# Transposes of the state prefix collected into two runs per head group, in an eight-core attention and mixture-of-experts layer

## What is computed

```python
x = x + attn(layernorm(x));  x = x + ffn(layernorm(x))
# attn: 32 heads of 64, blocks of 256 tokens
q, k, v = split(silu(h @ qkv_w.T))
def step(state, blk):                     # scan over the blocks
    aw = einsum('id,jd->ij', qi, ki) * dd
    y  = aw @ vi + (qi * qd) @ state
    state = state * bd + (ki * kd).T @ vi
    return state, y
attn = sigmoid(h @ gate_w.T) * rmsnorm(ys) @ out_w.T
# ffn, for each of 7 experts and a shared one:
u = xt @ Wup + bup;  g = silu(u @ Wgate + bgate) * u
out += probs * (g @ Wdown + bdown)        # probs: softmax over the top 2
```

## Time and profile before

| | us |
|---|---|
| runs of the kernel | 4628.54 and 4684.06, median 4656.3 |
| the profiled execution | 4629.22 |
| its span, on core 5, the slowest | 4627.2 |
| spans of the eight cores | 4614.4 to 4627.2 |
| mean granted TensorE clock | 0.908 to 0.910 |
| one group of the attention (208.9 to 488.2) | 279.3 |

### The profile page before, as it was taken

How to read it: one execution, slowest core, us unless ns; L and a number is a source line. 1 busy time by engine, 2 the same in 40 slices (tenths; PEclk the granted TensorE clock), 3 DMA queues, 4 the chain that set the end, 5 groups by cost and what they waited for, 6 DMA issues and landing times.

```text
span 4627.2 us, 44136 instructions; the slowest of 8 cores (4614.4 to 4627.2 us)
## 1 busy us (share of the span) xinstructions
PE 3923.8 (85%) x18010; PEld 1748.3 (38%) x18010; DVE 827.4 (18%) x1373; ACT 593.8 (13%) x691; POOL 249.9 (5%) x477
## 2 busy tenths in 40 slices
PE   1386867769659954999999999999999999999996
PEld 0132332324214411444444444444444444444443
DVE  3313122230322234011011011011010010110012
ACT  3311111111121030110110100100100100100100
POOL 0000000000000000000000000000000000000000
PEclk9996876869659966999999999999999999999997
DMA  3211110121104311444444444444444444444443
GB/s 101 72 32 19 33 32 19 28 46 33 23 5 73 69 45 25 76 73 75 76 73 76 75 73 74 77 73 74 76 75 74 73 73 73 74 74 76 78 69 96
DMA packets 75331, 284.48 MB, mean 61 GB/s; under 512 B 9814, under 2 KB 9975, under 8 KB 71038
## 3 DMA queue, kind: packets, MB, share of 16 engines
q0 software_dynamic: 67216, 243.39, 31.2%
q1 hardware_dynamic: 7918, 38.29, 2.6%
HBM read 516.55 MB, written 8.39 MB: 113 GB/s over the span
## 4 chain that ended last, share of the span: by engine, by line
PE 82%; DVE 8%; issue 4%; ACT 3%; DMA 2%; DVEq 0%; ACTq 0%; SPq 0%; POOL 0%; POOLq 0%
PE PD L368 28%; PE PE L368 27%; PE PE L1041 10%; PE PD L1041 10%; PE PT L383 2%; DVE awT L640 2%; PE PC L654 1%; PE PE L654 1%; DVE statc L405 1%; PE PC L1077 1%; PE PC L812 1%; ACT R L447 1%; DMA ring<-i_wup 1%; ACT R L674 1%; PE PC L665 0%
## 5 line engine op out<-in xcount | busy, mean ns | idle before, releaser
L368 PE MATMUL PD<-R,ring 128*128 128x512 bf16 x5888 | 1323.8, 384 | 23.7 <-ACT R L998 10.8
L368 PE MATMUL PE<-R,ring 128*128 128x512 bf16 x5888 | 1300.8, 379 | 2.2 <-DMA ring<-i_wgt 1.2
L368 PEld LDWEIGHTS PD<-R,ring 128*128 128x128 bf16 x5888 | 577.8, 99 | 738.4 <-issue 70.5
L368 PEld LDWEIGHTS PE<-R,ring 128*128 128x128 bf16 x5888 | 575.7, 98 | 698.2 <-issue 5.6
L1041 PE MATMUL PD<-R,ring 128*128 128x512 bf16 x2048 | 463.2, 385 | 24.9 <-DVE R L1025 21.0
L1041 PE MATMUL PE<-R,ring 128*128 128x512 bf16 x2048 | 452.5, 379 | 1.6 <-DMA ring<-i_wdn 1.6
L1018 DVE TENSOR_TENSOR R<-R 128x1024 bf16<-128x1024 bf16 x128 | 88.6, 692 | 1629.7 <-ACT R L1011 1629.7
L1041 PEld LDWEIGHTS PD<-R,ring 128*128 128x128 bf16 x2048 | 201.7, 99 | 278.2 <-issue 46.6
L1041 PEld LDWEIGHTS PE<-R,ring 128*128 128x128 bf16 x2048 | 199.5, 98 | 245.6 <-issue 7.3
L998 ACT ACTIVATE R<-PD,bupP 128x1024 bf16<-128x1024 f32 x56 | 62.4, 1114 | 1052.6 <-PE PD L368 929.6
L383 PE MATMUL PT<-ident_b,R 128*128 128x128 bf16 x256 | 37.4, 300 | 154.8 <-ACT R L447 120.1
(11 more groups left out here) (168 smaller groups left out, 1626.6 us busy)
## 6 DMA issues: line engine op xcount, KB each, us to landing
ring<-i_wup POOLq DMA_DIRECT2D x112, 512.0 KB, 5.1
ring<-i_wgt POOLq DMA_DIRECT2D x112, 512.0 KB, 5.2
ring<-i_wdn POOLq DMA_DIRECT2D x112, 512.0 KB, 5.1
xstage<-i_xm SPq DMA_DIRECT2D x16, 1024.0 KB, 5.1
ring<-i_wk POOLq DMA_DIRECT2D x16, 512.0 KB, 5.7
xstage<-i_xp SPq DMA_DIRECT2D x8, 1024.0 KB, 5.6
ring<-i_wv POOLq DMA_DIRECT2D x16, 512.0 KB, 5.7
ring<-i_wq POOLq DMA_DIRECT2D x16, 512.0 KB, 5.5
```

The source lines that it names most:

```text
L368: t.matmul(P[:, hh * 512:(hh + 1) * 512], sl[:, kc * 128:(kc + 1) * 128], rb[:, kc * 1024 + hh * 512:kc * 1024 + (hh + 1) * 512], start=st ...
```

## The change

The pairs are no longer issued one by one. The K loop only collects its eight batches in `pend`. They are issued together in the first turn of the V loop, between the R1 pass and the R2 pass of that slab (the R2 pass is the first to write into tmp_fm again). The V loop then collects its own eight batches, and they are issued behind the loop. No instruction is added or removed.

```diff
             project(slab, skey, R1, "R1", k_fm, ("kf", g, mcl), mcl * 1024)
             evp = project(slab, skey, R2, "R2", tmp_fm, ("tm", mcl), mcl * 1024)
-            for th in pend:
-                th()
-            pend = [lambda q4=q4, mcl=mcl, evp=evp: transpose_batch(
+            pend += [lambda q4=q4, mcl=mcl, evp=evp: transpose_batch(
...
             project(slab, skey, R1, "R1", q_fm, ("vmain", g, mcl), mcl * 1024)
+            if mcl == 0:
+                for th in pend:
+                    th()
+                pend = []
             evp = project(slab, skey, R2, "R2", tmp_fm, ("tm", mcl), mcl * 1024)
-            for th in pend:
-                th()
-            pend = [lambda q4=q4, mcl=mcl, evp=evp: transpose_batch(
+            pend += [lambda q4=q4, mcl=mcl, evp=evp: transpose_batch(
```

## The result

The changed kernel takes 4662.09 us (median of 11 runs; before 4657.8 in 10 runs taken with them). Both lists hold runs in which the cores of a die were given a lower clock, so medians compare badly; the runs free of it are 4656.6 to 4662.1 (six, with 4662.09 the highest) against 4625.5 to 4631.6 (five), a ratio of 1.0066 with an interval of 1.0052 to 1.0080. That is 31 us (24 to 37) more, less than the 2% that separate a change from none. The spans of the profiled executions agree: the slowest core 4657.1 against 4627.2, the mean of the eight cores 4652.2 against 4619.6, 32.6 more.

What follows compares the result with a forecast made beforehand. TensorE, busy 85%, was taken as the bound, through its order and waits. Per group 9.09 + 1.8 + 5.32 - 8.12 = 8.09 us, four groups 32.4, on 4629.2 gives 4662 us; range 4642 to 4716.

Steps and rivals of the forecast that it cites:

- The seam: Pair of transpose batches between two projection passes: 1.38 us of TensorE (1.30 for first pairs); six removed, 8.12 us per group.
- The K run: Eight batches between V0's R1 and R2 passes: 9.09 us added per group, 8.89 if the fourth batch is fast.
- The restart: R2 pass behind K's eight batches starts at the low clock: 1.8 us more per group, from rows of 1.16 to 2.54.
- The end of V: Eight batches instead of four before the key decay multiplies; the added four at low clock cost 5.32 us per group.
- The DMAs, ScalarE and VectorE at nothing: Ring loads, evictions and copies around the moved batches stay covered by passes, so they were costed at nothing.
- The clock that stays up through the K run: Rival: K's eight batches stay at full clock, no restart; 4651 us, or 4647 if V's end is fast too; chance 0.08.
- The clock that stays down longer: Rival: further passes behind K's eight batches at half clock, up to 6.91 us each; from 4722 us on; chance 0.04.
- The dearer seam: Rival: interrupting passes costs more than the rows show, so removal pays; 4629 us or less; chance 0.04, shared with no effect.

Runs made afterwards that it cites:

- e2_v_only: Kernel before with only V's eight batches collected and issued behind the V loop, K's pairs left as they were; ratio 1.0022 to before.
- e4_filler: Changed kernel with three unused matmuls in each of the seven waits among K's eight batches; mean span 4640.8 us, 11.4 less than the changed kernel.
- e5_after_two_pt: Changed kernel with transpose batches going in turn to PT and the first bank of PA; ratio 0.9799 to before.
- e7_spread: Kernel before, one PT, each pair's two batches issued inside the next slab's R1 pass; mean span 4598.6 us, 21.0 less than before.
- e3_fours: Kernel before with the list emptied when it holds four batches, behind K2, V0, V2 and at the end; ratio 1.0038 to before.

## Why the prediction was right

*The seam.* 1.38 us each, taken from the earlier trace rows, was right: pairs taken away in e2_v_only brought 1.34 each, and passes without seams between them stayed at 6.91.

*The K run.* 9.09 us, or 8.89 with a fast fourth batch, was put down; it takes 8.83 on core 6. The clock held for four batches there, in all four groups, not for three, and the first step is 0.07 shorter. Over the eight cores it held for four batches in 15 of the 32 K runs and for five in 17, which then take 8.62 us. Against before, seams and runs grew by (35.3 - 32.6) / 4 = 0.7 per group, where 9.09 - 8.12 = 1.0 was put down.

*The restart.* I took 1.8 us from rows behind other slow stretches. It was the worst known term, and it came out at 2.60, 2.63, 2.72 and 1.12 in the four groups of core 6. Over the 32 K runs it is 1.06 to 2.79, 1.97 in the mean. Over all restarts and cores the change is 22.8 - 14.9 = 7.9, or 2.0 per group. The term was a little small.

*The end of V.* Put down as 5.32; 4.86 in the group shown and (63.5 - 43.0) / 4 = 5.1 in the mean. The clock held here for five batches, and so one of the added ones was fast.

*The DMAs, ScalarE and VectorE at nothing.* Nothing in the trace contradicts it: in the projections of the attention no matmul waits for a ring load on any core, and behind the K run and at the end of V the same releasers stand with the same waits (6.92 us for the multiplies), and the three columns of the table leave 1.5 us of 32.6 to everything else.

*The rivals.* The clock that stays up through the K run fell on the trace (0.50 in the windows above); e4_filler shows what it would have been worth, 6 to 11 us. The Trainium skill's rule on it (TensorE: Matmul & The Clock Gate, Part 4, PE-mode transpose), that transpose mode doesn't count as activity in the same way, agrees with this fall, which followed all 32 K runs. It is not enough to tell when the clock falls: the first four to five batches after dense work ran at the high clock, and in e5_after_two_pt, where the batches stand closer, eight of them left it high in 24 of 32 runs. The clock that stays down longer did not come: the pass after the slow one takes 6.91. The dearer seam is excluded by e2_v_only and e7_spread. The sum was 32.4 us and the spans moved by 32.6; measured less predicted is -0.3 us per group in the runs of K and the seams, +0.2 in the restarts, -0.2 at the end of V and 1.5 us in all outside the three, so that closeness is in part luck. That 4662 meets the 4662.09 of the result to a tenth is luck altogether: the sum was put on the 4629.2 us of one execution, and the ratio stands for 31 us with 24 to 37 as its interval.

## What to carry to other kernels

Collecting short dependent steps into one long run is no saving when the engine gives them the same buffer: each step keeps its wait, and the only waits that cost nothing are those that lie beside dense work. Count the seams that have such work behind them, and those that don't. A second buffer for the steps (0.45 us a pair for 1.38) or a place inside a dense pass (0.44) removes the wait; both before any regrouping.

## What the runs showed of the hardware

The clock can fall after the waiting is over: in e3_fours it was 1.00 through four batches and 0.59 in the first 3.3 us of the pass behind them, and of twelve equal runs three or four are followed by that. Restarts cost from 0.5 to 2.9 us per slow pass in these kernels (only passes of over 7.3 us are counted), and the same place costs different amounts on different cores of one execution. Terms of this kind can be had from a trace as a range, not as a number.

Three unused matmuls of 0.22 us in each wait keep the clock at its high level in all 32 K runs and make the kernel 6 to 11 us faster. Closing the waits does it less surely: with two buffers eight batches take 4.1 us and 8 of 32 runs are followed by a slow pass, with one buffer four batches take 3.6 us and 25 of 96 are.

The column of the granted clock can't be trusted ahead of the first change that is recorded. In the kernel before it is 1.00 for the opening 208 us, though four transposes take 0.58 us there, as they do elsewhere at 0.50; the first pass (9.18 us to the next) is slow as well. The duration of a known instruction is the surer sign.

Windows of the kernel before:

```profile
0.00:208.00 208.00, 37.38 (x254) 22.36 (x254) 72.15 (x145) 74.70 (x97) 1.94 (x7) 1.00 0.34 94
```

and its timeline:

```profile
208.52 0.58 PE L383 MATMUL PT<-ident_b,R 128*128 128x128 bf16 x4 [0.75 <-DVE R L389]
208.90 9.34 PE L368 MATMUL PD<-R,ring 128*128 128x512 bf16 x32
```
